# Normalisation on ScalarE, gate folded into the output weights, two value projections moved one head group earlier

## The chip, the cores and the metric

One core of a Trainium2 chip. The metric is the device time of one execution in microseconds. The kernel before took 1692.3 us (median of three, 1688.98 to 1693.27).

## The reference

One transformer block with adaptive layer normalisation, for 8 batches of 1024 tokens and 256 channels. The modulation (`c`, 8x256, `wmod`, 256x1536) gives six rows for each batch: shift, scale and gate of both halves.

```python
mod = (silu(c) @ wmod).reshape(8, 6, 1, -1)
sa, ca, ga, sb, cb, gb = ...                       # gates are kept at |g| >= 0.25
h = layernorm(x) * (1 + ca) + sa
x = x + ga * (causal_attention(h) @ w_out.T + b_out)   # 16 heads of 16 channels
h = layernorm(x) * (1 + cb) + sb
x = x + gb * mix(h)
# mix: xr, xk = h and the token before, blended by mu; r = sigmoid(xr Wr'); out = r * (relu(xk Wk')^2 Wv')
```

## The kernel before

Tokens lie on the 128 partitions, 8 tiles a batch. The five engines run one static program each, in order, and meet at semaphores. A batch is worked in four head groups (`s` = 0 to 3, four heads each), a group in 12 steps (`t` = 0 to 11). In each step TensorE issues

1. row scores for the NEXT group (`row_ps`, four banks), of which VectorE takes the row maximum (`maximum`, L877);
2. column scores of this group (`col_ps`, two banks), of which ScalarE takes the exponential (`exps`, L715) into `weights`; on diagonal tiles GpSimd then masks (`select`, L604);
3. the value product of the step before (`val_ps`, L1137);
4. whatever dense unit the tables place at this step. All dense units share one PSUM bank, `dense_ps`: `claim_dense` waits until the unit before has been emptied (`free[...]`).

Three batches are in flight: the front of batch b+1, the attention of batch b, the back (output projection and mixing) of batch b-1. The tables that place dense units are

```python
V_STEPS, QK_STEPS, T_STEPS = (0, 1, 3, 9), (4, 5, 7, 8), (3, 5, 7, 9)
BACK_UNITS = ("out", "norm", "recept", "key", "value")
BACK_STEPS = dict(zip(BACK_UNITS, (2, 6, 10, 11, 13)))
```

`V_STEPS` are in group 0 of the batch that attends: unit k projects tiles 2k and 2k+1, ScalarE copies it into `v_ones` one step later (L736). `T_STEPS` are in group 1: the front's four transposes of normalised tokens (`xn_a`) of the next batch. `QK_STEPS` are in group 2 (chunk 0, next batch) and group 0 (chunk 1). Each group also takes one quarter (256 tokens) of the back of batch b-1, whose steps `u` count from the group's start up to 15, so that "value" falls into step 1 of the next group. Group 3 holds back units only.

The front's norm: VectorE `layernorm_stats` (end of step t-2 for a transpose at t), GpSimd `rstd` (step t-1: `var` L596, then a power, L598), VectorE `layernorm_apply` (end of step t-1: `xn = (x - mean) * rstd`, L913, two instructions of 128x256), TensorE transposes (L1166), ScalarE `h_full` and `h_hi` with shift and scale (L755, L758), GpSimd `h_lo` (L617). Shift and scale stand in `mod_front`, which VectorE copies out of `mod_t` in step 0 of group 1 (L922); `mod_back` likewise in step 0 of group 0 (L993).

The back's norm is the same in steps u = 4 (statistics), 5 (`rstd`, `layernorm_apply`), 6 (transposes), 7 (ScalarE, L770). Before it: u = 1 ScalarE `o_hi` (L787), u = 2 GpSimd `o_lo` (L627) and `xb` (residual + gate*bias, L636), TensorE the output product, u = 3 VectorE `gated = dense_ps * gate` (L960, frees the bank) and `xq = xq + gated` (L997).

GpSimd also makes the low parts `mix_lo` (L656) and `k_lo` (L660), and at u = 15 scales and adds the mixing result and issues its store. SyncE's queue issues, at the start of a group, 12 copies into the score stacks (L458), then (group 0) the gate rows, then the residual quarter (L501), then values and maxima.

After the last batch comes a drain: 31 steps in which the four last quarters run with a lag of five steps. Ahead of the first batch stands a preamble: weights are loaded and split (`w_hi` on ScalarE, L690, `w_lo` on VectorE, L830), and the first front is run alone.

## Time and profile before

| | us |
|---|---|
| profiled execution, its own time | 1694.45 |
| its span, first to last instruction | 1692.7 |
| median of three runs | 1692.3 |
| TensorE busy | 1466.9 |
| VectorE busy | 1127.2 |
| ScalarE busy | 940.6 |
| GpSimd busy | 625.6 |
| mean granted TensorE clock (share of full) | 0.883 |

A batch in the middle lasts 188 to 192 us; the preamble 88, the drain 107. Group boundaries below are the starts of ScalarE's first copy of `val_ps` in a group (L723). In tables by stretch each engine has its busy time and its count of instructions; PEclk is the granted clock, 1.00 at 2.4 GHz and 0.50 at 1.2 GHz.

### The profile page before, as it was taken

What the parts mean: (1) busy time and instruction counts of PE and PEld (TensorE: products, weight loads), DVE (VectorE), ACT (ScalarE), POOL (GpSimd) and SP (SyncE); (2) the same over time, 40 slices, a digit from 0 to 9 for tenths busy, and PEclk for the clock granted to TensorE, in tenths of its full rate; (3) what the DMA queues carried; (4) which work ended last, traced back from release to release, by engine and by line L of the source; (5) the groups of instructions that cost most, each with busy time, mean ns of one, the idle gap of its engine ahead of it and who ended that gap; (6) DMA issues with size and microseconds to landing.
All of it is one profiled execution on the core that took longest, in us unless ns stands there. A gap on an engine that the chain in (4) does not pass through costs nothing.

```text
span 1692.7 us, 30093 instructions
## 1 busy us (share of the span) xinstructions
PE 1466.9 (87%) x10856; PEld 832.6 (49%) x10856; DVE 1127.2 (67%) x2246; ACT 940.6 (56%) x1859; POOL 625.6 (37%) x752
## 2 busy tenths in 40 slices
PE   3798989889998999899898999899998999988653
PEld 2454435445554545555454545545554545543353
DVE  4667667876678766876678676876778777763320
ACT  2056555565666656566566566566666666655321
POOL 3002112443335333453335343453325333433454
PEclk7688889899998989989998999899998999987656
DMA  3221113121321213222221123221321223120200
GB/s 106 55 70 42 42 48 104 53 55 52 102 70 35 58 50 108 58 55 52 80 84 42 50 60 108 57 54 52 102 72 34 57 59 86 51 61 14 71 7 19
DMA packets 79828, 102.96 MB, mean 61 GB/s; under 512 B 22576, under 2 KB 43320, under 8 KB 79680
## 3 DMA queue, kind: packets, MB, share of 16 engines
q1 hardware_dynamic: 76544, 91.86, 20.1%
q0 software_dynamic: 2560, 8.39, 1.3%
q8 instruction: 86, 1.41, 0.4%
q10 hardware_dynamic: 576, 0.79, 0.2%
q14 instruction: 62, 0.51, 0.1%
HBM read 31.74 MB, written 8.94 MB: 24 GB/s over the span
## 4 chain that ended last, share of the span: by engine, by line
PE 58%; DVE 11%; POOL 9%; ACT 8%; issue 6%; SPq 5%; DMA 3%; ACTq 0%; POOLq 0%; DVEq 0%
PE col_ps L1068 14%; PE val_ps L1137 13%; PE row_ps L1105 8%; PE dense_ps L1147 7%; PE dense_ps L1148 5%; PE dense_ps L1149 5%; ACT weights L715 5%; DVE max_a L877 4%; SPq L458 4%; POOL weights L604 2%; PE row_ps L1116 2%; PE dense_ps L1166 2%; DMA xq<-in_x 2%; POOL mix_lo L656 1%; ACT h_hi L758 1%
## 5 line engine op out<-in xcount | busy, mean ns | idle before, releaser
L715 ACT ACTIVATE weights<-col_ps 128x512 f32<-128x512 f32 (+2 forms) x1280 | 643.1, 554 | 423.4 <-PE col_ps L1068 409.2
L877 DVE TENSOR_REDUCE max_a<-row_ps 128x1 f32<-128x512 f32 (+3 forms) x896 | 535.8, 644 | 219.3 <-PE row_ps L1116 129.5
L1068 PE MATMUL col_ps<-q_stack,k_stack 64*128 64x512 f32 (+3 forms) x1536 | 428.7, 443 | 36.7 <-ACT weights L715 34.8
L1105 PE MATMUL row_ps<-k_stack,q_stack 62*128 62x512 f32 (+3 forms) x1536 | 369.5, 435 | 24.6 <-DVE max_a L877 17.9
L1137 PE MATMUL val_ps<-weights,v_ones 128*32 128x512 f32 (+3 forms) x3072 | 359.9, 543 | 27.3 <-POOL weights L604 26.2
L604 POOL TENSOR_SCALAR_AFFINE_SELECT weights<-weights 128x512 f32<-128x512 f32 x256 | 165.0, 645 | 555.5 <-ACT weights L715 554.2
L1068 PEld LDWEIGHTS col_ps<-q_stack,k_stack 64*128 64x128 f32 x1536 | 205.6, 201 | 311.5 <-ACT weights L715 276.7
L877 DVE TENSOR_REDUCE max_b<-row_ps 128x1 f32<-128x384 f32 (+3 forms) x384 | 214.0, 595 | 148.3 <-PE row_ps L1116 148.2
L1105 PEld LDWEIGHTS row_ps<-k_stack,q_stack 62*128 62x128 f32 x1536 | 184.3, 203 | 134.8 <-DVE max_a L877 55.2
L1116 PE MATMUL row_ps<-mask_fill,mask_ident 64*128 64x128 bf16 (+1 forms) x2048 | 146.9, 217 | 0.0
L1137 PEld LDWEIGHTS val_ps<-weights,v_ones 128*32 128x32 f32 x3072 | 62.8, 112 | 121.4 <-issue 62.1
L1116 PEld LDWEIGHTS row_ps<-mask_fill,mask_ident 64*128 64x128 bf16 x2048 | 80.3, 101 | 33.5 <-issue 17.7
L649 POOL TENSOR_TENSOR h_diff<-h 128x512 f32<-128x512 f32 x32 | 33.3, 1041 | 156.6 <-ACT h L770 155.9
L656 POOL TENSOR_TENSOR mix_lo<-mixed,mix_hi 128x512 fp32r<-128x512 f32 x64 | 80.9, 1285 | 4.3 <-ACT mix_hi L793 4.2
L976 DVE SCALAR_TENSOR_TENSOR mixed<-h_diff,mus,h 128x256 f32<-128x256 f32 x128 | 61.7, 544 | 30.0 <-POOL h_diff L649 30.0
L1147 PE MATMUL dense_ps<-w_hi,mix_hi 128*128 128x256 f32 x128 | 42.0, 328 | 31.1 <-POOL mix_lo L656 29.2
L1147 PE MATMUL dense_ps<-h_hi,w_hi 128*128 128x512 f32 x128 | 61.6, 482 | 8.0 <-POOL h_lo L617 3.7
L660 POOL TENSOR_TENSOR k_lo<-k_sq,k_hi 128x512 fp32r<-128x512 f32 x32 | 47.0, 1468 | 46.2 <-ACT k_hi L798 46.2
L777 ACT ACTIVATE mix_out<-dense_ps 128x512 f32<-128x512 f32 x32 | 19.1, 598 | 76.0 <-PE dense_ps L1149 76.0
L1147 PE MATMUL dense_ps<-w_hi,k_hi 128*128 128x256 f32 x128 | 41.3, 322 | 18.8 <-POOL k_lo L660 12.9
L1148 PE MATMUL dense_ps<-h_lo,w_hi 128*128 128x512 f32 x128 | 54.3, 424 | 0.0
L1166 PE MATMUL dense_ps<-ident,xn_a 128*128 128x128 f32 x128 | 28.6, 362 | 29.2 <-DVE gated L960 11.7
(123 smaller groups left out, 2128.5 us busy)
## 6 DMA issues: line engine op xcount, KB each, us to landing
q_stack<-q_part SPq DMA_DIRECT2D x384, 64.0 KB, 2.2
k_stack<-k_part SPq DMA_DIRECT2D x372, 64.0 KB, 2.2
xa<-in_x SPq DMA_DIRECT2D x8, 1024.0 KB, 7.0
att<-val_out SPq DMA_DIRECT2D x64, 128.0 KB
recips<-recip_rows SPq DMA_DIRECT2D x32, 256.0 KB
xq<-in_x SPq DMA_DIRECT2D x28, 256.0 KB, 3.4
out<-xq POOLq DMA_DIRECT2D x28, 256.0 KB, 2.6
q_stack<-max_rows SPq DMA_DIRECT2D x256, 4.0 KB
```

What stands on the lines that cost most here:

```text
L458: sp.dma_start(stack[buf][at:at + HD, half].bitcast(F32), parts[part][lo:lo + 32, cols].bitcast(F32)).then_inc(stack_filled[buf][half], 16)
L604: nc.gpsimd.affine_select(out=w, in_=w, compare_op=ALU.is_ge, fill=0.0, base=0, pattern=[[0, G], [1, P]], channel_multiplier=-1).then_inc( ...
L656: nc.gpsimd.tensor_tensor(mix_lo[:, m], mixed[:, m], mix_hi[:, m].bitcast(F32), ALU.subtract).then_inc(mix_lo_done, 1)
L715: nc.scalar.activation(weights[:, t % 2, heads[0]:heads[-1] + 1:2, 0:q1 - q0], col_ps[bank][:, 0:n * (q1 - q0)].rearrange("p (h q) -> p h ...
L877: nc.vector.reduce_max(dest, bank[:, 0:len(heads) * (k1 - k0)].rearrange("p (h k) -> p h k", h=len(heads)), AX_X).then_inc(max_done, 1)
L1068: last = nc.tensor.matmul(col_ps[bank][:, i * (q1 - q0):(i + 1) * (q1 - q0)], stack_at(k_stack[s % 2], rows, heads[i], P * j, P * (j + 1)) ...
L1105: last = nc.tensor.matmul(banks[odd][:, n * width:(n + 1) * width], stack_at(q_stack[stack], rows, heads[n], P * i, P * (i + 1)), stack_at ...
L1116: last = nc.tensor.matmul(banks[odd][:, (n + 1) * width - P + ROW_TILE * a:(n + 1) * width], mask_ident[rows, a, :], mask_fill[rows, a, RO ...
L1137: last = nc.tensor.matmul(val_ps[32 * h:32 * h + 32, q0 - base:q1 - base], v_ones[:, j, G * s + h].rearrange("p d a -> p (d a)"), weights[ ...
L1147: nc.tensor.matmul(dst, a_hi(c), b_hi(c), start=(c == 0), stop=False)
L1148: nc.tensor.matmul(dst, a_hi(c), b_lo(c), start=False, stop=False)
L1149: last = nc.tensor.matmul(dst, a_lo(c), b_hi(c), start=False, stop=(c == KC - 1))
```

## The change

Four things.

- The normalisation is applied by ScalarE: `xn = rstd * x + shift` with `shift = -mean * rstd`, two ACTIVATEs of 128x256 that read SBUF. GpSimd's `rstd` makes the shift with two more instructions on 128x2 tiles. ScalarE issues them at the end of the same step in which VectorE did.
- Shift and scale of the modulation are read from `mod_t` in place; the copies `mod_front` and `mod_back` go.
- The attention gate is multiplied into the output weights once a batch, by GpSimd in step 6 of group 3 (three instructions of 128x512). VectorE adds `dense_ps` straight into the residual (one instruction in place of two), and for that waits for `xb` before it frees the bank. The gate rows are loaded in group 3 of the batch before, not in group 0. `w_out` is no longer part of the weights that the preamble splits.
- Value projections 0 and 1 of a batch run in steps 7 and 9 of the preceding group 3; the other two at steps 0 and 3 of group 0.

```diff
-V_STEPS, QK_STEPS, T_STEPS = (0, 1, 3, 9), (4, 5, 7, 8), (3, 5, 7, 9)
+V_EARLY, V_STEPS, QK_STEPS, T_STEPS = (7, 9), (0, 3), (4, 5, 7, 8), (3, 5, 7, 9)
-W_QK, W_V, W_O, W_R, W_K, W_F = 0, 1024, 1536, 2048, 2560, 3072
-W_ALL = 3584
+W_QK, W_V, W_R, W_K, W_F, W_O = 0, 1024, 1536, 2048, 2560, 3072
+W_FIXED, W_ALL = 3072, 3584
-        gated = sb("gated", [P, 2, D])
+        gated = xn_a
...
             if s == 0 and attends(kind):
                 if t in V_STEPS:
-                    k = V_STEPS.index(t)
+                    k = 2 + V_STEPS.index(t)
                     return "v", k, b * 4 + (k + 1)
...
+            if s == G - 1 and fronts(kind) and t in V_EARLY:
+                k = V_EARLY.index(t)
+                return "v", k, b * 4 + (4 + k + 1)
...
             def load_gates(b):
-                hold(x1_done, quarters(b, 0))
+                hold(xb_done, b * G)
                 sp.dma_start(gates_att[:].rearrange("p a n -> p (a n)"),
-                             gate_rows[bass.ds(b - 1, 1), 0:2 * D].partition_broadcast(P)).then_inc(gates_att_in, 16)
+                             gate_rows[b:b + 1, 0:2 * D].partition_broadcast(P)).then_inc(gates_att_in, 16)
...
-                    if backs(kind) and s == 0:
-                        load_gates(b)
...
                         place_max(q_stack[s % 2], 1)
+                    if attends(kind) and s == G - 1:
+                        load_gates(b)
...
-            def rstd(var, mv, out_t, mv_done, var_done, rstd_done, count):
+            def rstd(var, mv, out_t, shift, mv_done, var_done, rstd_done, shift_done, xn_done, count):
                 wait_apart(pool, "pool", mv_done, count)
+                wait(pool, xn_done, count - 1)
+                nc.gpsimd.tensor_scalar(shift[:], mv[:, :, 0], -1.0, None, ALU.mult)
                 nc.gpsimd.tensor_scalar(var[:], mv[:, :, 1], EPS, None, ALU.add).then_inc(var_done, 1)
                 pool.wait_ge(var_done, count)
                 nc.gpsimd.tensor_tensor(out_t[:], var[:], neg_half[:], ALU.pow).then_inc(rstd_done, 1)
+                pool.wait_ge(rstd_done, count)
+                nc.gpsimd.tensor_tensor(shift[:], shift[:], out_t[:], ALU.mult).then_inc(shift_done, 1)
...
+            def gate_out_weights(b):
+                pool.wait_ge(gates_att_in, (b + 1) * 16)
+                pool.wait_ge(ready["transposed"], b * 4 + (8 if b < B - 1 else 4))
+                wait(pool, w_out_done, b)
+                g = gates_att[:, 0:1, :].broadcast_to([P, KC, D])
+                nc.gpsimd.tensor_tensor(gated[:], w_out[:], g, ALU.mult).then_inc(w_gated, 1)
+                pool.wait_ge(w_gated, b + 1)
+                wait(pool, ready["out"], b * G)
+                hi, lo = (w[:, W_O:W_ALL].rearrange("p (k n) -> p k n", k=KC) for w in (w_hi, w_lo))
+                nc.gpsimd.tensor_copy(hi, gated[:]).then_inc(w_out_hi_done, 1)
+                pool.wait_ge(w_out_hi_done, b + 1)
+                nc.gpsimd.tensor_tensor(lo, gated[:], hi.bitcast(F32), ALU.subtract).then_inc(w_out_done, 1)
...
+                    if t == 6 and s == G - 1 and attends(kind):
+                        gate_out_weights(b)
...
-                        wait(act, val_done, val_index(b, 0, 0))
+                    last_use = val_index(b, 0, 0) if k >= 2 else val_index(b, G, 0)
+                    wait(act, val_done, last_use - (6 - 2 * k if k < 3 else 0))
...
+            def normalise(src, rstd, shift, dst, shift_done, done, count):
+                act.wait_ge(shift_done, count)
+                for i in range(2):
+                    last = nc.scalar.activation(dst[:, i, :], src[:, i, :], ACT.Identity, bias=shift[:, i:i + 1],
+                                                scale=rstd[:, i:i + 1])
+                last.then_inc(done, 1)
...
+            def normalise_next(b, kind, s, t):
+                if s == 1 and fronts(kind) and t + 1 in T_STEPS:
+                    ...
+                    wait(act, ready["transposed"], count - 1)
+                    normalise(xa[:, 2 * k:2 * k + 2, :], rstd_a, shift_a, xn_a, shift_a_done, xn_a_done, count)
...
+                if u == 5:
+                    wait(act, ready["norm"], q)
+                    normalise(residual(b, s), rstd_c, shift_c, xn_c, shift_c_done, xn_c_done, q + 1)
...
-            def layernorm_apply(src, mv, rstd, dst, rstd_done, done, count):
-                ...
-                if t == 0:
-                    nc.vector.tensor_copy(mod_front[:], mod_t[:, bass.ds(b * 8 + 8, 4)]).then_inc(mod_a_done, 1)
...
                 if u == 3:
+                    xr = residual(b, s)
+                    dve.wait_ge(xb_done, q + 1)
                     dve.wait_ge(ready["out"], q + 1)
-                    ga = gates_att[:, 0:1, :].broadcast_to([P, 2, D])
-                    nc.vector.tensor_tensor(gated[:], dense_ps[:], ga, ALU.mult).then_inc(free["out"], 1)
+                    nc.vector.tensor_tensor(xr, xr, dense_ps[:], ALU.add).then_inc(free["out"], 1)
...
-                    nc.vector.tensor_tensor(xr, xr, gated[:], ALU.add).then_inc(x1_done, 1)
...
                 if name == "out":
                     pe.wait_ge(o_lo_done, count)
+                    if s == 0:
+                        pe.wait_ge(w_out_done, b)
```

ScalarE's issue of the first keys' copies (`fill_first_keys`) moves from the end of the preamble's front to step 0 of its group 3, ahead of the early value copies.

## Rows read from the trace of the kernel before

**Rows 1.** The page, part 1: busy time, share of the span, instructions.

```profile
PE 1466.9 (87%) x10856; PEld 832.6 (49%) x10856; DVE 1127.2 (67%) x2246; ACT 940.6 (56%) x1859; POOL 625.6 (37%) x752
```

**Rows 2.** Windows of preamble, fourth batch and drain: us, busy by engine, PEclk, DMA, GB/s.

```profile
0.00:88.00 88.00, 47.86 (x208) 30.95 (x208) 49.57 (x99) 14.80 (x23) 18.42 (x28) 0.68 0.28 81
646.10:837.30 191.20, 176.46 (x1353) 99.45 (x1354) 140.29 (x279) 116.58 (x233) 77.13 (x92) 0.92 0.24 65
1585.50:1692.70 107.20, 49.67 (x220) 43.74 (x220) 25.54 (x55) 21.92 (x40) 51.65 (x52) 0.63 0.08 28
```

**Rows 3.** Windows of sixth batch, head groups 0 to 3, columns as above.

```profile
1026.50:1075.40 48.90, 47.21 (x387) 28.92 (x386) 34.61 (x68) 30.46 (x60) 17.33 (x20) 1.00 0.32 92
1075.40:1128.50 53.10, 46.37 (x332) 24.34 (x329) 41.92 (x87) 32.91 (x69) 26.16 (x32) 0.81 0.18 49
1128.50:1174.30 45.80, 43.23 (x338) 24.73 (x336) 32.34 (x65) 27.90 (x56) 16.87 (x20) 0.96 0.20 54
1174.30:1214.40 40.10, 36.57 (x310) 19.92 (x308) 29.90 (x62) 25.50 (x53) 16.87 (x20) 1.00 0.27 72
```

**Rows 4.** Waits of TensorE in head group 1: us, times, longest us.

```profile
PE col_ps L1068 <- ACT weights L715: 2.0, 4, 0.7
PE dense_ps L1147 <- POOL o_lo L627: 1.0, 1, 1.0
...
PE dense_ps L1166 <- DVE xn_a L913: 0.4, 1, 0.4
```

**Rows 5.** Waits of the whole span, the same columns.

```profile
PE row_ps L1105 <- DVE max_a L877: 17.9, 24, 1.0
...
PE dense_ps L1166 <- DVE gated L960: 11.7, 6, 2.5
```

**Rows 6.** Groups of instructions by line, the whole span.

```profile
L668 POOL TENSOR_TENSOR mix_out<-mix_out,gates_mix 128x512 f32<-128x512 f32 x32 | 41.0, 1282 | 14.6 <-DVE mix_out L965 14.6
...
L913 DVE TENSOR_SCALAR xn_a<-xa,mv_a,rstd_a 128x256 f32<-128x256 f32 x64 | 35.8, 601 | 6.1 <-POOL rstd_a L598 6.1
...
L598 POOL TENSOR_TENSOR rstd_c<-var_c,neg_half 128x2 f32<-128x2 f32 x32 | 23.2, 724 | 2.7
...
L913 DVE TENSOR_SCALAR xn_c<-xq,mv_c,rstd_c 128x256 f32<-128x256 f32 x56 | 20.5, 409 | 4.2 <-POOL rstd_c L598 4.2
...
L787 ACT ACTIVATE o_hi<-att_n 128x512 fp32r<-128x512 f32 x32 | 20.1, 628 | 6.4 <-PE dense_ps L1149 6.4
...
L997 DVE TENSOR_TENSOR xq<-xq,gated 128x512 f32<-128x512 f32 x28 | 19.6, 698 | 0.0
...
L922 DVE COPY mod_front<-mod_t 128x4 f32<-128x4 f32 x8 | 7.8, 974 | 0.0
```

**Rows 7.** Timeline of VectorE, start of group 1.

```profile
1086.06 2.77 DVE L913 TENSOR_SCALAR xn_a<-xa,mv_a,rstd_a 128x256 f32<-128x256 f32 x2
...
1089.36 0.68 DVE L960 TENSOR_TENSOR gated<-dense_ps,gates_att 128x512 f32<-128x512 f32 x1
```

**Rows 8.** Timeline of ScalarE, middle of group 1.

```profile
1102.43 2.28 ACT L715 ACTIVATE weights<-col_ps 128x512 f32<-128x512 f32 x4
1104.93 1.02 ACT L770 ACTIVATE h<-dense_ps,mod_back 128x256 f32<-128x256 f32 x2 [0.22 <-PE dense_ps L1166]
```

**Rows 9.** Timeline of TensorE in group 0: a value projection, then the next product.

```profile
1030.46 0.39 PE L1147 MATMUL dense_ps<-w_hi,h_hi 128*128 128x256 f32 x1
...
1032.87 0.38 PE L1147 MATMUL dense_ps<-w_hi,k_hi 128*128 128x256 f32 x1 [0.73 <-ACT v_ones L736]
```

**Rows 10.** Timeline of ScalarE in group 3.

```profile
1193.83 1.09 ACT L715 ACTIVATE weights<-col_ps 128x512 f32<-128x512 f32 x2 [0.82 <-PE col_ps L1068]
```

**Rows 11.** Timeline of ScalarE in the preamble.

```profile
15.45 3.19 ACT L690 ACTIVATE w_hi<-v_ones 128x3584 fp32r<-128x3584 f32 x1 [7.31 <-DMA v_ones<-in_w_v_t]
...
31.52 1.02 ACT L755 ACTIVATE h_full<-dense_ps,mod_front 128x256 f32<-128x256 f32 x2 [1.44 <-POOL h_lo L617]
```

**Rows 12.** Timeline of VectorE in the drain.

```profile
1597.99 2.58 DVE L913 TENSOR_SCALAR xn_c<-weights,mv_c,rstd_c 128x256 f32<-128x256 f32 x2 [0.91 <-POOL rstd_c L598]
```

More of the change, by code:

```diff
@@ L147, in build @@
         mod_t = sb("mod_t", [P, B * 8])
-        mod_front = sb("mod_front", [P, 4])
-        mod_back = sb("mod_back", [P, 4])
+        w_out = sb("w_out", [P, KC, D])
         gates_att = sb("gates_att", [P, 2, D])
@@ L801, in body @@
                 for s, t, at in timeline(b, kind):
+                    if kind == "first" and (s, t) == (G - 1, 0):
+                        fill_first_keys()
                     front(b, kind, s, t)
@@ L829, in _ @@
             dve.wait_ge(w_hi_done, 1)
-            nc.vector.tensor_tensor(w_lo[:], w_raw, w_hi[:].bitcast(F32), ALU.subtract).then_inc(setup_done, 1)
+            nc.vector.tensor_tensor(w_lo[:, 0:W_FIXED], w_raw, w_hi[:, 0:W_FIXED].bitcast(F32), ALU.subtract).then_inc(setup_done, 1)
             dve.wait_ge(mod_ready, 1)
@@ L908, in layernorm_stats @@
                 last.then_inc(mv_done, 1)
-            def layernorm_apply(src, mv, rstd, dst, rstd_done, done, count):
-                dve.wait_ge(rstd_done, count)
-                for i in range(2):
-                    last = nc.vector.tensor_scalar(dst[:, i, :], src[:, i, :], mv[:, i, 0:1], rstd[:, i:i + 1],
-                                                   ALU.subtract, ALU.mult)
-                last.then_inc(done, 1)
             def front(b, kind, s, t):
@@ L991, in back @@
                                             ).then_inc(att_done, 1)
[L992 to L994 removed]
+                if u == 4:
                     dve.wait_ge(free["out"], q + 1)
[L996 to L1003 removed]
+                    layernorm_stats(xr, stats_c, mv_c, stats_c_done, mv_c_done, shift_c_done, q + 1)
             def body(b, kind):
```

69 lines of the change are left out of this document (29 added, 40 removed).

## The prediction

> **What bounds the kernel now.** I read the page's busy shares first, then the stretches of the span, then one batch by head group, then what TensorE waits for, and last the timelines of the places that the edit touches. The page has TensorE as the busiest engine and no other near it [rows 1]. By stretch the seven or eight batches make the time, 188 to 192 us each, and TensorE is busy for 176 of 191 us in one; preamble and drain are chains of small steps at a low granted clock [rows 2]. A batch is not even. Group 0 has the most matmuls, runs at the full clock and leaves TensorE 1.7 us idle: TensorE bounds it. Group 1, with the front's norm and transposes, has the fewest but one, and is the longest: VectorE is busy 41.9 of 53.1 us, TensorE idle 6.7 us, and the granted clock is 0.81, a mixture of the 2.4 and the 1.2 GHz level. Group 3 is the lightest, with 3.5 us of TensorE idle [rows 3]. So there is something to win at group 1 (VectorE's work) and by levelling groups 0 and 3. Within group 1 the dearest wait of TensorE is the one for `gated`, which stands behind the first `xn_a` on VectorE [rows 5, 7]; the other waits are for the exponentials, for `o_lo` and for the last `xn_a` [rows 4].
>
> The sum is made against the profiled execution's 1694.45 us, 2.2 us above the median of 1692.3.
>
> **Norm off VectorE.** 64 + 64 instructions leave it: 601 ns for `xn_a`, 409 ns for `xn_c` [rows 6], 8 us of its 139 us in a batch. The mean of 601 hides two levels: the first pair of group 1 took 2.77 us [rows 7], twice 1.4, while GpSimd was running operations of 1.28 us. The Trainium skill has a rule for this (SBUF — State Buffer, Who interferes with whom): VectorE in a two-port mode and GpSimd exclude each other for a whole instruction, and ScalarE has a port of its own; this trace agrees, by 2.77 us against 0.8 for two of 409 ns. The part on the path: in the sixth batch `xn_a` ends at 1088.83, one row maximum follows, and `gated` frees the bank at 1090.04; TensorE had waited 2.5 us for it by then [rows 5, 7]. There are six such waits, one in each batch that has a front and a back, 11.7 us in all [rows 5], 1.95 each. With the pair gone from ahead of it all of that goes. `mod_front` (974 ns, [rows 6]) leaves VectorE ahead of the statistics; GpSimd's `rstd`, behind which `o_lo` is queued, gets longer by the shift. Net 0.5 us of the 1.0 us wait for `o_lo` [rows 4]. Together -2.4 a batch (0 to -4). The last `xn_a` wait, 0.4 us [rows 4], goes too: in step 8 ScalarE is ahead of VectorE. Row maxima for which TensorE waits, 17.9 us in all [rows 5], 2.2 a batch: a fifth of it, as VectorE loses a tenth of its work, -0.4. `mod_back` and the gate rows' issue ahead of the residual load: -0.2. The second residual instruction (698 ns x 4, [rows 6]) lies beside TensorE's work in the batches and costs nothing there; the new wait for `xb` in front of the freeing add is covered by the output product itself, since `xb` (1.28 us) runs while the 12 matmuls do; uncovered, where a residual load is late, it would cost up to 1 us in group 3, where nothing needs the bank before step 6.
>
> **Norm on ScalarE.** The same work as two ACTIVATEs. Nearest rows: a pair from PSUM with scale and bias columns, 1.02 us [rows 8]; above, two of `o_hi`, which reads SBUF, 128x512, 628 ns: 1.26 us [rows 6]. I take 1.08, as it is nearest to the first. Eight pairs a batch, 8.6 us on an engine that is busy 117 of 191 us [rows 2]. What matters is what they stand in front of: ScalarE is strictly in order and TensorE has only two `col_ps` banks, so an exponential late by x makes the next column scores late by x unless value or row products cover it. First pair of group 1: ScalarE waits for TensorE there, free. Last one (step 8): free. Second: after the copy of step 4, nearly free. The third and the quarter's pair fall into steps 5 to 8, where ScalarE has `h_full`, `h_hi`, `h` and four exponentials a step and is idle 0.22 us between them [rows 8]; 1.08 - 0.22 = 0.86 each, less what the products cover: +1.4. In groups 0, 2 and 3 one pair each ahead of step 6, where ScalarE idles 0.82 us once a step [rows 10]: between 0.26 and 1.08, I take 0.35: +1.0. Together +2.4 a batch (0.5 to 8.6).
>
> GpSimd: one instruction like `var` and one product of 128x2; the only row of that form is the power, 724 ns [rows 6], the upper end; lower end 0.2; I take 0.45 us for both. It delays `h_diff` or `o_lo` behind it by as much and is counted above. ScalarE would wait for the shift only where GpSimd is late; in steady batches GpSimd itself waited for VectorE's statistics.
>
> The Trainium skill speaks against this part (ScalarE: Activation LUTs, Rules for kernel authors): multiplications and additions belong on VectorE. By that page's figures (186 ns, 93 for each column operand, 0.833 ns an element, 93 of overlap) a pair is an estimated 1.08 us, so the sum stays as it is; what it warns of is the second rival.
>
> **Gate in the weights.** Three GpSimd instructions of 128x512 once a batch, at most 3 x 1.28 [rows 6] = 3.9 us, in step 6 of group 3. GpSimd idles there (16.9 of 40.1 us busy, [rows 3]) until `h_diff` of step 8, and the product that needs them is a dozen steps off; their cover gone they would delay `h_diff` by 1 us. SyncE's queue now holds for the third `xb` in group 3 before it stores values of step 4, which come later anyhow. Nothing.
>
> **Value projections.** One occupies TensorE from 1030.46 to 1032.14, 1.7 us, and the next product then waits 0.73 us for its copy [rows 9]. Two leave group 0, which TensorE bounds: -3.5 (2 x 1.6 less overlap, plus the wait). They enter group 3, where TensorE is idle 3.5 us [rows 3]; half of their time is hidden: +1.6, and their two copies on ScalarE add +0.4. Net -1.5 a batch (-3.5 to 0).
>
> **Sum.** A full batch: -2.4 - 0.4 - 0.4 - 0.2 + 2.4 - 1.5 = -2.5; six of them -15. Batch 0 has no back, -1. Batch 7 has no front: -3.5 + 1.4 - 0.2 = -2.3. Preamble: `w_hi` shrinks by a seventh (3.19, [rows 11]), `w_lo` as well, one load goes: -1.5; but the first front is a chain: the next transposes used to run while ScalarE waited 1.44 us for `h_lo` [rows 11], and now norm (1.08) and transposes (1.1) stand there one after the other: +0.9 three times, +0.6 for the first, +0.5 for the early projections, which meet a stretch that VectorE's maxima bound: +2 net. Drain: `xn_c` 2.58 [rows 12] becomes 1.08 and one 0.7 us addition goes, the shift costs 0.3: -1.9; in the three later quarters ScalarE stands waiting for the shift ahead of the tanh that TensorE needs, +0.3 each: -1. Total -15 - 1 - 2.3 + 2 - 1 = -17.3: 1677.2 on the profiled execution's scale, 1675 on the median's. Forecast 1676, with its own range 1664 to 1686, chance 0.46.
>
> **Rivals.**
> - The half-clock stretches shrink as well. Group 1 ran 332 matmuls in 46.4 us of TensorE time, group 2 338 in 43.2 [rows 3]; at group 2's rate 42.5, so 3.9 us a batch more. For: the gap ahead of the transposes lies just before such a stretch. Against: steps 5 to 8 get new gaps. Full effect 6 x 3.9 = 23 us: 1653; half 1664. Chance 0.18.
> - ScalarE becomes the bound and it ends slower. Place: steps 4 to 7 of every group, the exponentials behind a norm pair. Price: if 7 of the 8.6 us of pairs in a batch are exposed, a full batch is -2.5 + 4.6 = +2.1, six +12.6, with the rest about +15: 1708; all 8.6 exposed +26: 1720. It decides from 5.1 us exposed in a batch. For: ScalarE's 0.22 us of idle [rows 8] and TensorE's waits for exponentials, 2.0 us in group 1 [rows 4], already the second of its kind. Against: 39% of the time ScalarE is idle. Chance 0.22.
> - Gains and losses cancel: the projections are not hidden in group 3 (+1.6) and the pairs cost 3.5: -2.5 + 1.6 + 1.1 = 0.2 a batch: 1692. Chance 0.14.
>
> A measurement of this kernel can tell about 0.3% (5 us) from no change. Faster by more 0.64, within 0.13, slower 0.23. The range of 8 in 10 is 1652 to 1706: below by the full clock effect, above by most of the ScalarE case.
>
> **What would show it.** Right: VectorE busy 8 to 12 us less a batch, ScalarE 8 to 9 more; no wait of transposes on VectorE in group 1; group 0 shorter by 3 to 4 us, group 3 longer by 1 to 3, group 1 shorter by 1 to 3; waits of TensorE for L715 up from 2.0 to some 3.5 us in group 1. Wrong: group 1 as long as before or longer, waits on the exponentials up by 4 us or more (second rival); PEclk of group 1 above 0.9 (first rival); group 3 longer by over 3 us (third). A pair of ACTIVATEs over 1.26 us, a late `xb` that holds the bank, or SyncE's hold in group 3 delaying values would be mistakes of my terms.

## The result and the profile after

The changed kernel takes 1680.5 us in the median (20 runs, 1670.9 to 1693.2), the kernel before 1690.8 (20 runs): ratio 0.9943, 95% interval 0.9923 to 0.9963, so 0.6% faster. Beside the experiments it was timed again: 1677.9 against 1689.9, ratio 0.9947 (0.9923 to 0.9971). The profiled execution is 1685.1 us, its span 1683.4.

The page's busy shares after, against [rows 1]:

```profile
PE 1455.4 (86%) x10856; PEld 829.5 (49%) x10856; DVE 1039.4 (62%) x2070; ACT 997.8 (59%) x1987; POOL 677.3 (40%) x904
```

VectorE lost 88 us of work, ScalarE took 57, GpSimd 52. TensorE has the same 10856 matmuls and is busy 11.5 us less: the same work at a higher clock. The sixth batch by head group, group 0 first, against [rows 3]; the columns are the stretch, its length, busy time and instructions of TensorE, its weight loads, VectorE, ScalarE and GpSimd, granted clock, DMA share, GB/s:

```profile
1026.90:1073.00 46.10, 44.40 (x364) 26.39 (x364) 32.43 (x64) 30.00 (x61) 17.69 (x22) 1.00 0.33 90
1073.00:1123.50 50.50, 42.45 (x331) 23.05 (x329) 34.92 (x75) 37.18 (x79) 28.17 (x42) 0.93 0.20 51
1123.50:1167.70 44.20, 41.66 (x338) 23.86 (x335) 30.78 (x62) 28.63 (x58) 17.30 (x22) 1.00 0.22 56
1167.70:1210.50 42.80, 39.82 (x335) 22.70 (x332) 28.75 (x59) 27.87 (x56) 20.39 (x25) 1.00 0.28 75
```

Group 0 is 2.8 us shorter, group 3 2.7 longer, group 1 2.6 shorter with 3.9 us less of TensorE time and a granted clock of 0.93 instead of 0.81. TensorE's waits in that group 1, against [rows 4] and the wait for `gated` in [rows 5]; the columns are total, times and longest, in us:

```profile
PE col_ps L1090 <- ACT weights L742: 3.3, 4, 1.6
PE val_ps L1159 <- POOL weights L615: 2.0, 3, 1.1
PE dense_ps L1169 <- POOL o_lo L653: 1.0, 1, 1.0
PE row_ps L1127 <- DVE max_a L923: 0.8, 1, 0.8
PE dense_ps L1169 <- POOL k_lo L685: 0.5, 1, 0.5
PE dense_ps L1188 <- DVE xq L991: 0.2, 1, 0.2
```

The 2.5 us for `gated` are 0.2 now. The exponentials took 1.3 more, and GpSimd's causal selection (`weights` L615) 2.0 where it was 0.8. So the waits were exchanged, not removed. The shift is not the cause of the longer wait for the selection: e2 and e6 below have the same four GpSimd instructions, and TensorE waits 1.0 us for it there. The other rows are those of group 1 in batches 1, 2, 3, 4 and 6:

```profile
318.20:368.20 50.00, 43.14 (x331) 22.80 (x327) 35.08 (x75) 37.47 (x78) 28.32 (x42) 0.90 0.20 51
507.20:558.50 51.30, 44.52 (x331) 23.40 (x329) 35.03 (x75) 37.14 (x79) 28.19 (x42) 0.87 0.19 48
697.40:746.40 49.00, 40.97 (x332) 21.85 (x329) 34.99 (x75) 37.29 (x79) 28.18 (x42) 0.97 0.19 48
885.00:934.10 49.10, 40.87 (x331) 21.66 (x328) 34.95 (x75) 37.25 (x79) 28.18 (x42) 0.97 0.19 49
1257.00:1305.90 48.90, 40.94 (x332) 21.73 (x329) 35.02 (x75) 37.32 (x79) 28.19 (x42) 0.97 0.21 53
```

The same view of before gives a mean of 52.5 us with 45.0 us of TensorE time; the first and the last of its six:

```profile
311.60:363.80 52.20, 43.85 (x330) 23.16 (x327) 41.70 (x87) 32.69 (x68) 26.32 (x32) 0.87 0.18 47
...
1263.30:1315.30 52.00, 43.97 (x332) 23.43 (x329) 41.94 (x87) 32.82 (x69) 26.16 (x32) 0.87 0.19 50
```

After, the mean is 49.8 us with 42.1 us of TensorE time. TensorE's idle time stayed: 7.5 us before, 7.7 after. All of the 2.7 us is in its busy time. Twice (1 - PEclk) times the length is the time at 1.2 GHz: 15.8 us a group before, 6.5 after.

Two places lost. The first front, in the timeline of ScalarE (start, us, instruction, in brackets the idle time before and its releaser), is one loop of norm, transposes, `h_full`, `h_hi`, 4.17 us a turn where before it was 3.37:

```profile
30.41 1.09 ACT L792 ACTIVATE xn_a<-xa,shift_a,rstd_a 128x256 f32<-128x256 f32 x2
32.76 1.02 ACT L781 ACTIVATE h_full<-dense_ps,mod_t 128x256 f32<-128x256 f32 x2 [1.27 <-PE dense_ps L1188]
33.68 1.02 ACT L784 ACTIVATE h_hi<-dense_ps,mod_t 128x256 fp32r<-128x256 f32 x2
34.58 1.09 ACT L792 ACTIVATE xn_a<-xa,shift_a,rstd_a 128x256 f32<-128x256 f32 x2
```

ScalarE's first copy of values comes at 112.8 us instead of 106.6. The clock has no part in that: in the second trace of the changed kernel (e12 below), with 68 us at 1.2 GHz ahead of this copy instead of 31, it comes at 113.0. And the drain is 110.2 us instead of 107.3. In ScalarE's timeline the norm waits for GpSimd, and the tanh for which TensorE waits (`mix_out`, L817) stands behind it, in both quarters shown.

```profile
1600.26 1.09 ACT L792 ACTIVATE xn_c<-weights,shift_c,rstd_c 128x256 f32<-128x256 f32 x2 [3.67 <-POOL shift_c L609]
1601.26 0.58 ACT L817 ACTIVATE mix_out<-dense_ps 128x512 f32<-128x512 f32 x1
...
1623.35 1.09 ACT L792 ACTIVATE xn_c<-weights,shift_c,rstd_c 128x256 f32<-128x256 f32 x2 [9.65 <-POOL shift_c L609]
1624.35 0.57 ACT L817 ACTIVATE mix_out<-dense_ps 128x512 f32<-128x512 f32 x1
```

TensorE's waits for the tanh in the drain went from 2.7 to 5.4 us. They are 5.4 in each of the four traces with this norm on ScalarE in the drain, and 2.7 in the ten others. After, and then before:

```profile
PE dense_ps L1169 <- ACT mix_out L817: 5.4, 4, 1.6
```

```profile
PE dense_ps L1147 <- ACT mix_out L777: 2.7, 4, 0.7
```

GpSimd itself comes to the shift only after `mix_lo`:

```profile
1619.07 2.50 POOL L681 TENSOR_TENSOR mix_lo<-mixed,mix_hi 128x512 fp32r<-128x512 f32 x2
1621.66 0.24 POOL L604 TENSOR_SCALAR shift_c<-mv_c 128x2 f32<-128x2 f32 x1
1621.96 0.22 POOL L605 TENSOR_SCALAR var_c<-mv_c 128x2 f32<-128x2 f32 x1
1622.26 0.72 POOL L607 TENSOR_TENSOR rstd_c<-var_c,neg_half 128x2 f32<-128x2 f32 x1
1623.06 0.20 POOL L609 TENSOR_TENSOR shift_c<-shift_c,rstd_c 128x2 f32<-128x2 f32 x1
```

### The profile page after: what moved, and what is told of

Its sections match the earlier page's. It is cut to its first block, busy times and chain, and to the rows that moved or that the text cites. A ratio compares the mean times of both kernels' runs of the same rounds, so it can differ in the third digit from the quotient of the medians.

```text
span 1683.4 us, 30248 instructions
## 1 busy us (share of the span) xinstructions
PE 1455.4 (86%) x10856; PEld 829.5 (49%) x10856; DVE 1039.4 (62%) x2070; ACT 997.8 (59%) x1987; POOL 677.3 (40%) x904
## 4 chain that ended last, share of the span: by engine, by line
PE 57%; POOL 11%; DVE 9%; ACT 8%; issue 6%; SPq 5%; DMA 3%; ACTq 0%; POOLq 0%; DVEq 0%
PE col_ps L1090 14%; PE val_ps L1159 12%; PE row_ps L1127 8%; PE dense_ps L1169 7%; PE dense_ps L1170 5%; PE dense_ps L1171 5%; SPq L465 4%; ACT weights L742 4%; DVE max_a L923 4%; POOL weights L615 2%; PE row_ps L1138 2%; DMA xq<-in_x 2%; POOL mix_lo L681 2%; PE dense_ps L1188 2%; POOL mix_out L693 1%
## 5 line engine op out<-in xcount | busy, mean ns | idle before, releaser
L615 POOL TENSOR_SCALAR_AFFINE_SELECT weights<-weights 128x512 f32<-128x512 f32 x256 | 164.3, 642 | 553.4 <-ACT weights L742 552.2
L1159 PE MATMUL val_ps<-weights,v_ones 128*32 128x512 f32 (+3 forms) x3072 | 353.6, 534 | 34.7 <-POOL weights L615 34.6
L764 ACT ACTIVATE v_ones<-dense_ps 128x512 f32<-128x512 f32 x32 | 20.2, 631 | 63.4 <-PE dense_ps L1171 63.4
L1171 PE MATMUL dense_ps<-h_hi,w_lo 128*128 128x512 f32 x128 | 54.2, 423 | 0.0
```

Of the source, the lines that this page charges most:

```text
L615: nc.gpsimd.affine_select(out=w, in_=w, compare_op=ALU.is_ge, fill=0.0, base=0, pattern=[[0, G], [1, P]], channel_multiplier=-1).then_inc( ...
L1159: last = nc.tensor.matmul(val_ps[32 * h:32 * h + 32, q0 - base:q1 - base], v_ones[:, j, G * s + h].rearrange("p d a -> p (d a)"), weights[ ...
L1171: last = nc.tensor.matmul(dst, a_lo(c), b_hi(c), start=False, stop=(c == KC - 1))
```

## The experiments

They were timed in three sets of four (e1 to e4, e5 to e8, e9 to e12), each set on a chip of its own and beside the kernel before (medians 1691.6, 1692.5 and 1689.9). e3, e5, e9 and e10 have six executions, e6 eight, the others 11 or 12. The ratio is not the quotient of the two medians; the two differ by up to 0.26% (e6: 1.0071, and 1.0045 by the medians). Differences in microseconds between kernels of different sets are taken from the ratios below, and are good to some 5 us. The table has for each the median, the ratio with its interval, and from its one profiled execution the mean length of head groups 0 to 3 over batches 1 to 6, and in the last column how much of group 1 was at 1.2 GHz (in us; groups are cut at ScalarE's first copy of values). Two profiled executions of the changed kernel differ by 4.8 us over these six batches (1125.4 and 1120.6), so a total from one trace is worth no more than that; medians and ratios decide.

```
kernel              median  ratio (95%)              g0    g1    g2    g3   at 1.2 GHz
before              1690.8                           48.9  52.5  46.4  42.2  15.8
changed             1680.5  0.9943 (0.9923-0.9963)   46.4  49.8  46.4  45.0   6.5
changed, again e12  1677.9  0.9947 (0.9923-0.9971)   46.4  50.1  46.1  44.3   8.2
e1 V back           1679.9  0.9926 (0.9902-0.9950)   49.0  49.8  46.4  42.6   6.2
e2 norms on VectorE 1688.9  0.9985 (0.9960-1.0011)   46.1  53.5  46.2  43.8  18.2
e3 ends on VectorE  1671.7  0.9876 (0.9832-0.9920)   46.5  50.0  45.7  44.2   7.9
e4 V moved alone    1692.2  0.9996 (0.9968-1.0023)   46.9  52.6  45.4  43.9  15.3
e5 xn_a on ScalarE  1668.3  0.9883 (0.9849-0.9916)   46.1  49.3  46.3  44.6   7.9
e6 xn_c on ScalarE  1700.1  1.0071 (1.0041-1.0101)   46.1  55.5  45.8  44.0  18.7
e7 wait filled      1687.9  0.9991 (0.9961-1.0020)   49.1  52.1  46.6  43.0  10.4
e8 ends, V back     1680.3  0.9935 (0.9908-0.9961)   49.0  50.4  45.4  43.2   9.0
e9 combined         1667.6  0.9884 (0.9848-0.9921)   46.3  49.4  46.6  44.4   8.4
e10 comb., V back   1669.3  0.9891 (0.9852-0.9931)   49.0  49.4  46.4  42.6   8.6
e11 comb., no fold  1677.1  0.9941 (0.9910-0.9971)   46.9  50.9  46.7  43.8   9.6
```

What TensorE waits for in group 1 is steadier from trace to trace than a length. The mean of batches 1 to 6, in us; the first column is the wait for the instruction that frees the output product's bank (`gated` or `xq`), ahead of the transposes, and the last holds smaller waits too:

```
                    frees bank  xn_a  o_lo  exponentials  selection  row maxima  all
before                     1.9   0.3   1.5           2.2        0.8         0.0  7.4
changed                    0.2   0.0   1.0           3.1        2.1         0.6  7.4
changed, again e12         0.2   0.0   1.0           2.9        2.1         0.4  7.3
e1 V back                  0.2   0.0   1.0           3.0        2.1         0.8  7.6
e2 norms on VectorE        2.4   0.2   1.0           2.8        1.0         0.0  7.8
e3 ends on VectorE         0.2   0.0   1.0           3.0        2.1         0.6  7.5
e4 V moved alone           1.9   0.4   1.6           2.5        0.8         0.0  7.6
e5 xn_a on ScalarE         0.2   0.0   1.0           2.2        2.1         0.4  6.7
e6 xn_c on ScalarE         2.4   1.4   1.0           3.5        1.0         0.0  9.7
e7 wait filled             1.1   0.5   1.6           3.0        0.8         0.0  7.6
e8 ends, V back            0.2   0.0   1.0           3.0        2.1         0.4  7.3
e9 combined                0.2   0.0   1.0           2.3        2.2         0.1  6.7
e10 comb., V back          0.2   0.0   1.0           2.2        2.2         0.3  6.8
e11 comb., no fold         0.1   0.0   2.1           2.9        1.4         0.1  7.7
```

**e1: the moved projections undone.**

```diff
-V_EARLY, V_STEPS, QK_STEPS, T_STEPS = (7, 9), (0, 3), (4, 5, 7, 8), (3, 5, 7, 9)
+V_EARLY, V_STEPS, QK_STEPS, T_STEPS = (), (0, 1, 3, 9), (4, 5, 7, 8), (3, 5, 7, 9)
-                    k = 2 + V_STEPS.index(t)
+                    k = V_STEPS.index(t)
...
-                    last_use = val_index(b, 0, 0) if k >= 2 else val_index(b, G, 0)
+                    last_use = val_index(b, 0, 0)
```

> The changed kernel with all four value projections of a batch back in head group 0 (steps 0, 1, 3, 9); the rest of the change stays. The prediction's term says that the move is worth 1.5 us in a full batch and more in the last: group 0 gets 3.5 us longer again, group 3 2.0 us shorter, the preamble 0.5 to 2.5 us shorter; together 1680.5 + 9 + 3.5 - 2 = about 1691, ratio to the kernel before 0.998 to 1.001. Rival, read from the traces of before and after (group 0 gained 2.4 us, group 3 lost 2.7): the move is worth nothing in a full batch, and what it costs ahead of batch 0 comes back: about 1676 to 1681, ratio 0.991 to 0.994.

Measured 0.9926: the rival's case. Group 0 is 2.6 us longer, group 3 2.0 shorter (against the mean of the two traces of the changed kernel), group 1 as before the undoing. The gain of the change doesn't come from the projections.

**e4: the same edit alone**, made on the kernel before.

> The kernel before with only the two value projections moved to the preceding group 3. The prediction's term: -1.5 us in each of six batches, -3.5 in the last, +0.5 to +2.5 ahead of batch 0: 1690.8 - 11 = about 1680, ratio 0.993 to 0.995. Rival (a swap of equal times between group 0 and group 3): 1688 to 1693, ratio 0.999 to 1.002, group 0 shorter by 2.4 and group 3 longer by 2.4 or more.

Measured 0.9996: again nothing. Group 0 gives 2.0, group 3 takes 1.7.

**e2: both norms back on VectorE**, the rest of the change kept. ScalarE's `normalise` is called no more, and VectorE gets

```diff
+                if t + 1 in T_STEPS and (True):
...
+                    layernorm_apply(xa[:, 2 * k:2 * k + 2, :], mv_a, rstd_a, xn_a, rstd_a_done, xn_a_done, count)
...
+                if u == 5 and (True):
+                    wait(dve, ready["norm"], q)
+                    layernorm_apply(xr, mv_c, rstd_c, xn_c, rstd_c_done, xn_c_done, q + 1)
```

GpSimd still makes the shift, which nothing reads any more in e2; the same holds for the norms that are on VectorE in e3, e5, e6 and e8 to e10.

> The changed kernel with both normalisations back on VectorE, everywhere; gate in the weights, modulation in place and the moved projections stay. Theory of the sum: in the batches the norm on ScalarE gives the freed wait ahead of the transposes (2.0 us) and 0.8 us more, and costs 2.4 us of late exponentials, so taking it back costs only 0.3 us a batch (+2 us), while preamble and drain, where the norm stands in a chain on ScalarE, give back 3.3 us and 3 to 4 us: 1680.5 + 2 - 7 = about 1676, ratio 0.991. Rival one: the norm off VectorE is the source of all that head group 1 gained (2.7 us a batch): +16 - 7, about 1690, ratio 0.999. Rival two: late exponentials cost more than it gives, by 1 us or more a batch: 1667 or less, ratio below 0.987. Told apart by group 1 of batches 1 to 6: 50.1, 52.5 or under 49 us.

Measured 0.9985, rival one. Group 1 is at 53.5 us: the norm off VectorE makes the gain, and the rest of the change without it makes none that can be told from nothing (interval to 1.0011). What the idle shift costs in that is not separated. Group 1 of the sixth batch, and two of TensorE's waits in it:

```profile
1075.20:1128.20 53.00, 44.99 (x331) 23.92 (x329) 39.95 (x85) 32.73 (x69) 28.11 (x42) 0.84 0.19 48
```

```profile
PE col_ps L1105 <- ACT weights L742: 2.9, 4, 1.0
PE dense_ps L1203 <- DVE xq L1003: 2.4, 1, 2.4
```

The wait ahead of the transposes is back at 2.4 us though `gated` is gone: what is late is the instruction that frees the bank, whatever it writes, because `xn_a` is ahead of it.

**e5 and e6: one norm each.** In e5 `xn_c` is back on VectorE everywhere (the second hunk above), in e6 `xn_a` (the first).

> The changed kernel with the back's normalisation (the one that makes xn_c) on VectorE again, everywhere; the front's (xn_a) stays on ScalarE. Theory now: what counts is group 1, where xn_a on VectorE stood ahead of the instruction that frees the output product's bank, and where the granted clock fell behind that gap; xn_a is what matters. Then group 1 of batches 1 to 6 stays at 49.8 to 50.5 us with 5 to 9 us of it at the 1.2 GHz level, and the drain gets 3 us shorter: about 1678, ratio 0.991 to 0.994. Rival: the relief is that VectorE has less to do in all, whichever pair leaves; with half of the pairs back, group 1 is half way, 51.5 us with 12 us at the lower level: 1680.5 + 10 - 3 = 1687, ratio 0.998.

> The changed kernel with the front's normalisation (xn_a) on VectorE again, everywhere; the back's (xn_c) stays on ScalarE. Theory now: group 1 goes back to 52.5 to 53.5 us with 15 to 18 us at the 1.2 GHz level, the preamble gets 3.3 us shorter, the drain keeps its loss: 1680.5 + 18 - 3 = about 1695 with everything, ratio 1.000 to 1.003. Rival (less work on VectorE, whichever): half way, 51.5 us in group 1: 1687 or less, ratio 0.996 to 0.998.

The two norms are of opposite sign. With `xn_a` alone on ScalarE the kernel is at 0.9883, 10 us faster than with both; with `xn_c` alone at 1.0071, slower than before. Both went further than expected, e5 below its 0.991 and e6 above its 1.003. The place, on VectorE in e6, and GpSimd's timeline in the same microseconds:

```profile
1086.96 2.78 DVE L960 TENSOR_SCALAR xn_a<-xa,mv_a,rstd_a 128x256 f32<-128x256 f32 x2
1089.66 0.68 DVE L923 TENSOR_REDUCE max_a<-row_ps 128x1 f32<-128x512 f32 x1
1090.27 0.67 DVE L1003 TENSOR_TENSOR xq<-xq,dense_ps 128x512 f32<-128x512 f32 x1
```

```profile
1086.97 1.28 POOL L693 TENSOR_TENSOR mix_out<-mix_out,gates_mix 128x512 f32<-128x512 f32 x1
1088.33 1.26 POOL L695 TENSOR_TENSOR xq<-xq,mix_out 128x512 f32<-128x512 f32 x1
```

The pair lasts as long as GpSimd's two operations do. An estimate from these rows: 2.78 us less the 0.73 of an undisturbed pair are 2.05 of the 2.4 us for which TensorE waits, so that the place in VectorE's order matters because a slow pair stands there. The cheaper remedy, the pair behind the freeing addition but still on VectorE, was not tried. In e5 nothing stands there, and the freeing addition follows a maximum directly:

```profile
1071.48 0.69 DVE L923 TENSOR_REDUCE max_a<-row_ps 128x1 f32<-128x512 f32 x1 [0.38 <-PE row_ps L1142]
1072.09 0.68 DVE L1003 TENSOR_TENSOR xq<-xq,dense_ps 128x512 f32<-128x512 f32 x1
```

What `xn_c` costs on ScalarE: TensorE waits 0.7 to 0.9 us a batch longer for exponentials in group 1 (changed against e5, e3 against e9, e8 against e10), at most 0.3 longer in group 3, and no longer in groups 0 and 2. Against the two traces of the changed kernel e5 is 5.5 us shorter in batches 1 to 6 (1117.5 to a mean of 1123.0), with TensorE waiting 2.4 us for exponentials in the sixth group 1 instead of 3.3; its drain is 104.6 us instead of 110.2 and 107.4. There `xn_c` on VectorE lasts 0.73 us, off ScalarE's queue, and TensorE's waits for the tanh are the 2.7 us shorter:

```profile
1592.50 0.73 DVE L960 TENSOR_SCALAR xn_c<-weights,mv_c,rstd_c 128x256 f32<-128x256 f32 x2 [3.02 <-POOL rstd_c L607]
1611.42 0.74 DVE L960 TENSOR_SCALAR xn_c<-weights,mv_c,rstd_c 128x256 f32<-128x256 f32 x2 [6.86 <-POOL rstd_c L607]
1633.54 0.73 DVE L960 TENSOR_SCALAR xn_c<-weights,mv_c,rstd_c 128x256 f32<-128x256 f32 x2 [6.79 <-POOL rstd_c L607]
```

The rest of the drain's difference goes with the clock: granted 0.66 over e5's drain, 0.55 and 0.63 over the changed kernel's. e3, with the same drain as e5, was granted 0.63 and took 107.6.

In e6 more than the exponentials is worse than in e2: TensorE also waits 1.4 us instead of 0.2 for `xn_a`. Where that comes from was not followed.

**e7: the wait filled**, on the kernel before. TensorE repeats a pair of row products five times ahead of the first transposes; the result is the same.

```diff
-                for n in range(len(pair[0])):
+                for n in [m for _ in range(repeats + 1) for m in range(len(pair[0]))]:
...
-                    row_scores(b, s, late)
+                    row_scores(b, s, late, 5 if (s == 1 and t == 3 and kind in ("second", "mid")) else 0)
```

> The kernel before, in which TensorE computes the last pair of row products ahead of the first transposes of group 1 (step 3, batches 1 to 6) five times more into the same banks before it signals them: about 1.1 to 2.1 us of matmuls in the 2.5 us in which it otherwise waits for the output product's bank. No other engine's work changes. Theory that the clock makes the gain: with the idle time filled the stretch at the 1.2 GHz level behind it gets shorter, from 15.8 us of group 1 to some 6 to 10, and group 1 goes from 52.5 to 50 to 51 us although TensorE has more to do: 1690 - 9 to -15, ratio 0.991 to 0.995. Theory of the prediction, that the wait itself is the loss: the filling lies in the wait and changes nothing, or costs up to 1 us where the row maxima behind it come late: ratio 1.000 to 1.004, group 1 at 52.5 to 53.5 us.

Both theories missed a part. The ten additional matmuls take 1.15 us in the sixth batch, all of it inside the wait. With them the time at 1.2 GHz falls from 15.8 to 10.4 us a group, as the clock's theory has it, and TensorE's busy time falls too, from 45.0 to 44.4; but the group is only 0.4 us shorter and the kernel the same (0.9991). In the sixth batch:

```profile
1071.60:1124.20 52.60, 44.30 (x341) 23.87 (x337) 41.86 (x87) 32.93 (x68) 26.16 (x32) 0.90 0.18 47
```

```profile
PE col_ps L1068 <- ACT weights L715: 2.9, 4, 1.3
PE dense_ps L1148 <- POOL o_lo L627: 1.6, 1, 1.6
PE dense_ps L1167 <- DVE gated L960: 1.3, 1, 1.3
PE dense_ps L1167 <- DVE xn_a L913: 1.2, 1, 1.2
```

What TensorE no longer spends at the low clock it waits: over the six batches 0.8 us more for the exponentials (3.0 for 2.2), where 0.8 less are left at the freed bank; the other waits of this group changed by 0.2 at most. VectorE's 41.9 us of work in the group stand as they did. That a faster TensorE is worth something in group 1 only where VectorE is relieved too fits this and e5, and isn't shown by itself.

**e3 and e8: the two ends.** In e3 the norms of the first front and of the drain are on VectorE and batch 0 keeps its four projections in its own group 0; e8 has the norms so, and all projections in group 0.

```diff
-                if s == 1 and fronts(kind) and t + 1 in T_STEPS:
+                if s == 1 and fronts(kind) and t + 1 in T_STEPS and not (kind == "first"):
...
-                if u == 5:
+                if u == 5 and not (b == B):
```

> The changed kernel, but the four normalisations of the first front and the four of the drain are on VectorE, and batch 0 has its first two value projections in its own group 0 as in the kernel before. Theory: the first front's chain step falls from 4.17 back to 3.37 us (-0.8 four times), the early projections at half clock leave the preamble (-2.5, of which batch 0's group 0 takes up to 2.4 back), the drain's quarters fall from 23.1 to some 21.5 us (-3 to -4): 1680.5 - 6 to -9, about 1673, ratio 0.988 to 0.991. Rival: the start's loss of 8.6 us is the load order and the clock and not the chain, and the drain's is the wait for the reciprocals' transfer: both stay, 1680, ratio 0.994.

> The changed kernel with the first front's and the drain's normalisations on VectorE and all value projections back in group 0: gate in the weights, modulation in place and the norms of batches 0 to 7 on ScalarE stay. By the first four runs (projections worth nothing, the ends 8.8 us): 1671 to 1673, ratio 0.987 to 0.989. If the ends' gain in the earlier run came in part from the first two projections of batch 0 alone, no more than that run gave: 1672. If the moved projections are worth the 1.5 us a batch of the prediction once ScalarE is free at the ends: 1681, ratio 0.994.

e3 came as expected in its median: 1671.7, its first copy of values at 107.0 us instead of 112.8. Its drain, 107.6 us, is no shorter than that of the changed kernel's second trace (107.4), though. The four traces with the first front on ScalarE (the changed kernel twice, e1, e5) have that copy at 112.0 to 113.0, those with it on VectorE (e2, e3, e6, e8 to e11) at 104.8 to 111.5, mean 108.3: 4.2 us. e8 missed: 1680.3, no better than e1, though its trace has the early start (107.1) and the short drain (104.5). Its profiled execution, 1671.2 us, is the fastest of its twelve, so it doesn't show what the median lacks.

**e9, e10, e11: the sum of what was learned.** e9 leaves on ScalarE only `xn_a` of the fronts of batches 0 to 6; batch 0 has its projections in its own group 0. e10 is e9 with all projections in group 0. e11 is e9 with `gated`, its later addition, `mod_front` and `mod_back` as in the kernel before, and without GpSimd's three instructions on the output weights and its shift for `xn_c`.

> The changed kernel with the back's normalisation (xn_c) on VectorE everywhere, the first front's xn_a on VectorE too, and batch 0 with all its value projections in its own group 0; so ScalarE makes xn_a in the fronts of batches 0 to 6 only. Sum of the earlier runs: xn_c back gave 8 to 12 us, the first front's chain 3 to 5 us: 1663 to 1668, ratio 0.983 to 0.986. If the gain of the run with xn_c on VectorE was that of the drain alone and luck of six executions: 1672, ratio 0.988 to 0.990.

> The same, with all value projections of every batch in group 0. Two pairs of runs disagree on what the move is worth: nothing (the change with and without it, and the kernel before with and without it) or 8 us (with the norms of both ends on VectorE). Theory: nothing, because what leaves group 0 (2.4 us) comes back in group 3: the same time as the run before within 3 us. Rival: worth 1 to 1.5 us a batch once nothing else is late: 7 to 10 us slower than the run before, ratio 0.990.

> The combined version without the gate in the output weights and without the modulation read in place: VectorE multiplies the output product by the gate into a buffer of its own and adds it later, and the modulation columns are copied, as in the kernel before. Theory: the weight fold and the reading in place were worth little (the run with both norms on VectorE stood 0 to 0.3% from the one with the projections alone): 0 to 3 us slower than the combined version. Rival: the fold is what lets VectorE free the bank early: 8 us or more slower, group 1 above 51 us.

> The changed kernel as it is, beside the three others on one chip: 1680, ratio 0.993 to 0.996; the combined version should be 10 to 16 us faster than it.

e9 is 1667.6 us: 1.2% faster than the kernel before and some 10 us faster than the changed one beside it (1677.9). Its median is in the range that the sum gave, its ratio in that of the other theory. It is no better than e5 (0.9883), so the first front's 4 us don't show in the median. e10, 1669.3, is the same: the projections are worth nothing here either. In batches 1 to 6 of its trace e9 is 5.4 us shorter (0.9 a batch), but its last batch is 180.0 us against 173.9, with 34 us at 1.2 GHz in group 3 against 20. What the last batch does with early projections differs from pair to pair, though: 5 us longer in e3 than in e8, 4 us shorter in e4 than in the kernel before. So the traces don't say where the gain of the six batches goes.

e11 is 9.5 us slower than e9 (0.9941, its interval just above that of e9 but for the overlap from 0.9910 to 0.9921), with group 1 1.5 us longer and 38.0 us of VectorE's work there against 35.6. Its profiled execution is the slowest of its twelve, so its lengths are too long. Its waits show one cause: TensorE waits 2.1 us for `o_lo`, 1.0 in e9. In e11 VectorE copies `mod_front` ahead of the statistics, GpSimd waits for these, and `o_lo` stands behind GpSimd's `rstd`. The copy and GpSimd's start on the statistics in e11, and that start in e9:

```profile
1079.94 1.24 DVE L955 COPY mod_front<-mod_t 128x4 f32<-128x4 f32 x1
```

```profile
1084.28 0.24 POOL L623 TENSOR_SCALAR shift_a<-mv_a 128x2 f32<-128x2 f32 x1 [2.39 <-DVE mv_a L940]
```

```profile
1061.40 0.24 POOL L608 TENSOR_SCALAR shift_a<-mv_a 128x2 f32<-128x2 f32 x1 [1.24 <-DVE mv_a L958]
```

The wait for the freed bank is 0.1 us in e11 and 0.2 in e9. In group 1, then, the copied modulation is dear and the gate's own instruction is not; no run undoes one of the two alone, so what the fold of the gate is worth by itself stays open.

## Why the prediction was right in its range and wrong in its terms

It forecast 1676 with its own range of 1664 to 1686, 16 us less than the 1692.3 that it started from; the medians fell by 10.3 and, beside the experiments, by 12.0. It forecast -2.5 us in a full batch; six batches were to give -15, and the profiled ones gave -15.4 (1140.8 to 1125.4) and, in the second trace, -20.2. The stretches around them did not fit. Up to the start of batch 1 it had +1 (+2 and -1), and the trace has +8.7. The last batch had -2.3 and has -5.5. The drain had -1 and has +2.9. That the total fell in the range was thus in good part luck: the terms were wrong in both directions.

- **Head of group 1, -2.4.** The place and its price were right: over the six batches the wait for the freed bank fell from 1.9 to 0.2 us and that for `o_lo` by the 0.5 that the sum had, and e2 and e6 bring 2.4 us back by putting `xn_a` ahead of the freeing addition. But TensorE's idle time in group 1 did not fall (7.5 to 7.7 us). Selection (+1.3), exponentials (+0.9) and row maxima (+0.6, where the sum had -0.4) took over what the head gave. The step that failed is adding wait by wait: TensorE's and VectorE's waits here lie in one chain, and one removed wait passes on to the next.
- **The clock, 0 in the sum, rival one with 0.18.** It came: 15.8 to 6.5 us at 1.2 GHz. Its full effect, "at group 2's rate 42.5, so 3.9 us a batch more", was too high. Taken within each kernel, over the 84 executions of group 1 in 14 traces, a group with 1 us more at 1.2 GHz is 0.21 us longer (correlation 0.84); by that 9.3 us are 2.0 us of the 2.7. In e7 5.4 us less gave 0.4. That the clock is a cause and not only a sign is thus shown only in part.
- **Norm on ScalarE, +2.4 a batch.** Mis-sized, and laid on the wrong pairs. The price of a pair, 1.08 us, measured 1.09. What it costs TensorE is 0.7 to 0.9 us of waits for exponentials in group 1, all for the back's pair (with the front's pairs alone on ScalarE they are 2.2 us, as before), nothing in groups 0 and 2 and at most 0.3 in group 3, where +1.0 was put for the three. The front's pairs, given +1.4 by way of the third, pay for themselves many times: e5 against e2 is 0.9883 against 0.9985, -17 us. The back's pair was given +0.35 in three groups and nothing to win. In the whole kernel it costs 10 us by e5 against the changed kernel and 14 by e6 against e2. Undone in the batches alone, with the drain's already on VectorE, it gives 7 us in e10 against e8 and nothing in e9 against e3. The second rival's mechanism, a pair ahead of exponentials, is thus real for `xn_c`, at 0.9 us of waits a batch where it would decide from 5.1; and e6 ends on that rival's side, slower than before, in part by its wait for `xn_a`. The Trainium skill's advice to keep multiplications and additions on VectorE (ScalarE: Activation LUTs, Rules for kernel authors) holds here for `xn_c` and not for `xn_a`.
- **Value projections, -1.5 a batch.** By size and split nearly right in the six batches (-2.0 to -2.7 in group 0 instead of -3.5, and +1.1 to +2.4 in group 3; all groups together -0.9 a batch in e9 against e10, -1.4 in e4), wrong for the kernel: three pairs (the changed kernel and e1, e4 and before, e9 and e10) differ by about 0.2% or less, within their intervals. Where batch 0's are early, part is lost at the start: the copy in e4 comes 3.3 us later than in the kernel before. Where the rest goes isn't shown.
- **Gate in the weights, nothing.** The three GpSimd instructions (3.2 us together) delayed nothing: TensorE's waits for GpSimd's selection in group 3 are 1.2 us a batch in e1, which has the instructions, as before. Gate and modulation together gave nothing in e2 against e4 and 9.5 us in e11 against e9; of that the trace shows the wait for `o_lo`, which the sum had under VectorE's relief at 0.5.
- **Preamble, +2.** 6.2 us to the first copy. The chain was rightly seen (+3.3; measured 0.8 in each of three turns and 2.9 up to the last `h_hi`). The gain from the shorter `w_hi` (1.5) was not there: `w_hi` took 2.76 us instead of 3.19, but began 0.5 us later, with the load that it waits for. The early projections were mis-sized at +0.5: moved alone, in e4, they put the first copy back by 3.3 us. Of the two, one ran at 1.2 GHz (2.9 us) and one at 2.4 (1.7) in the changed kernel.
- **Drain, -1.** It was +3.0 in the first trace, +0.2 in the second. VectorE's `xn_c` took 0.73 us in the three later quarters, not the 2.58 of the first [rows 12]. TensorE's one wait for it fell by 1.7 us (6.8 to 5.1), and e5, with the same addition gone and the norm on VectorE, has 5.8, so that most of this would come without ScalarE. The norm ahead of the tanh, put at +0.3 in three quarters, cost +0.9 in each: 2.7 us. The rest follows the granted clock (0.63 before, 0.55 and 0.63 after).

The signs that it named fit so: VectorE lost 11 us a batch (8 to 12), ScalarE took 7 (8 to 9 named), and the granted clock of group 1 is above 0.9 in four of the six batches, the sign of the first rival. So -15 came out of terms of -1.5 for the projections (worth nothing in the end), -3.4 for VectorE's waits and +2.4 for ScalarE's, where the runs show 0, about -17 in the whole kernel for `xn_a` and up to +14 for `xn_c`.

**Open.** e3 and e8 differ by 0.6% (intervals 0.9832 to 0.9920 and 0.9908 to 0.9961) and only by the projections, which three other pairs find worth nothing; e3 has six executions. And e8 against e10, alike but for `xn_c` in the batches, differ by 0.4%, which fits the price of `xn_c`, while e3 against e9, which differ by the same, don't differ. One of e3 and e8 being off by luck would explain all of this; no run shows it.

## What to carry to other kernels

When work moves from one engine to another, ask it of each instance, not of the sum: the same operation won 17 us by leaving VectorE, where it stood ahead of an instruction that frees TensorE's bank and had GpSimd working beside it, and cost some 10 us where it came to stand in ScalarE's queue ahead of exponentials and, in the drain, of a tanh. TensorE's waits in a stretch where a second engine is nearly as busy are exchanged, not added up; read its idle time and its busy time apart, since a stretch with the same work, less busy time and the same idle time ran at a higher clock. Try each part of a change alone and with its partner: gate and modulation gave nothing without the norm's move and some 9 us with it, and the best versions, e5 and e9, leave one of the two norms where it was. And ask the trace which of two parts undone together made a wait: here it was not the one under suspicion.

## What the runs showed of the hardware

- A pair of 128x256 normalisations on VectorE took 0.73 us beside a quiet GpSimd and 2.78 us when it began with a GpSimd pair of 1.28 and 1.26 us; on ScalarE it took 1.09 us in every row shown. The slow pair ended within 0.2 us of GpSimd's. That agrees with the rule of the Trainium skill (SBUF — State Buffer, Who interferes with whom) that the port pair which the two share is an exclusive lock, and that ScalarE has ports of its own.
- A microsecond more at 1.2 GHz goes with a group 1 that is 0.21 us longer, a group 2 by 0.45 and a group 3 by 0.35 (84 executions of each, in 14 traces). It is least where VectorE is busiest (35 to 42 us of a group 1, 29 to 33 of the other two); that this is the reason wasn't tried. Group 0, hardly ever at 1.2 GHz, says nothing.
- More work can leave TensorE less busy: with 10 matmuls more in group 1 its busy time fell from 45.0 to 44.4 us, while the time at 1.2 GHz fell from 15.8 to 10.4.
- GpSimd's instructions on 128x2 values take 0.19 to 0.24 us, its power 0.72 us; the chain of four that makes `rstd` and the shift is 1.6 us. With both norms on VectorE and this chain kept (e2) TensorE waits 1.0 us for the causal selection in group 1, against 0.8 before.
